# Attention denominators: two exponential tiles added by an accumulating DMA, one pass of the small constant over the sum

## What is computed

```python
scores = jnp.einsum('bhtd,bhsd->bhts', q, k) / SCALE
scores = jnp.where(causal[None, None], scores, NEG_INF)
attn = jax.nn.softmax(scores, axis=-1)
mask = jnp.clip((R + z[:, :, None, None] - dist) / R, 0.0, 1.0)
attn = attn * mask
attn = attn / (attn.sum(axis=-1, keepdims=True) + 1e-08)
out = jnp.einsum('bhts,bhsd->bhtd', attn, v)
```

## Time and profile before

| | |
|---|---|
| median of three runs | 3301.56 us (3301.55 to 3304.24) |
| the profiled execution | span 3301.3 us; the median of the runs is 0.3 us above it |
| self-attention | from 355 to 1825 us of the span, some 1470 us in eight iterations |
| busy in the span | PE 91%, DVE 56%, ACT 32%, POOL 29% |

### The profile page before, as it was taken

One profiled execution on the slowest core, in us unless ns is written; L12 is line 12 of the kernel. 1 busy time (PEld: TensorE's weight loads), 2 busy tenths in 40 slices (PEclk: granted clock), 3 DMA queues, 4 the chain that ended last, 5 costly groups with the idle time before them and its releaser, 6 DMA issues. The chain is left out here.

```text
span 3301.3 us, 54795 instructions
## 1 busy us (share of the span) xinstructions
PE 2990.0 (91%) x19242; PEld 1673.0 (51%) x19242; DVE 1859.6 (56%) x2220; ACT 1063.0 (32%) x2510; POOL 943.3 (29%) x606
## 2 busy tenths in 40 slices
PE   8998799999999999999999789999999787777778
PEld 6876333333333333333333678888888343333335
DVE  4355878787887878787883345555554510000038
ACT  3222344444444444444444223333333100101123
POOL 0000554445444444445454022222222000000013
PEclk9999899999999999999999889999999888878889
DMA  4453512121212212131200411111111669999954
GB/s 166 178 204 128 128 49 62 51 70 44 70 53 55 69 48 60 52 73 43 69 16 4 150 42 64 64 64 64 64 64 65 243 249 420 420 421 420 421 226 162
DMA packets 181219, 438.54 MB, mean 133 GB/s; under 512 B 17470, under 2 KB 51928, under 8 KB 156457
## 3 DMA queue, kind: packets, MB, share of 16 engines
q1 hardware_dynamic: 174057, 425.19, 36.8%
q10 hardware_dynamic: 6976, 10.75, 0.9%
HBM read 351.74 MB, written 83.89 MB: 132 GB/s over the span
## 5 line engine op out<-in xcount | busy, mean ns | idle before, releaser
L785 ACT ACTIVATE B_e<-B_pS 128x512 f32<-128x512 f32 (+3 forms) x1280 | 619.2, 534 | 850.0 <-PE B_pS L865 427.9
L640 POOL TENSOR_TENSOR B_em<-B_e,B_mask 128x1024 f32<-128x1024 f32 (+1 forms) x320 | 670.9, 2098 | 730.7 <-ACT B_e L785 693.9
L703 DVE TENSOR_REDUCE mx<-B_pM 128x4 f32<-128x2048 f32 (+2 forms) x299 | 588.9, 1969 | 38.7 <-PE B_pM L847 20.3
L865 PE MATMUL B_pS<-B_qs,B_ks 128*128 128x512 f32 (+3 forms) x1280 | 505.2, 447 | 43.4 <-issue 19.7
L696 DVE SCALAR_TENSOR_TENSOR B_em<-B_mask,B_e 128x1024 f32<-128x1024 f32 (+1 forms) x320 | 354.4, 1108 | 257.9 <-PE B_pN L895 256.3
L865 PEld LDWEIGHTS B_pS<-B_qs,B_ks 128*128 128x128 f32 x1280 | 227.8, 192 | 363.1 <-issue 238.5
L883 PE MATMUL B_pD<-B_e,B_tiny 128*32 128x512 f32 (+3 forms) x2560 | 310.0, 557 | 0.0
L889 PE MATMUL B_pD<-B_em,B_ones 128*32 128x512 f32 (+3 forms) x2560 | 301.2, 543 | 0.3 <-DVE B_em L696 0.3
L895 PE MATMUL B_pN<-B_em,B_v 128*32 128x512 f32 (+3 forms) x2560 | 293.4, 530 | 0.0
L2089 PE MATMUL E_pI<-ring,hT 128*32 128x512 f32 x1024 | 184.5, 815 | 101.1 <-DMA ring<-in_L_ffn_e_W_dram 57.8
L2012 DVE TENSOR_TENSOR E_ug<-E_pT,bT 128x32 f32 x32 | 5.7, 192 | 445.2 <-PE E_pT L2099 445.2
(11 more groups left out here) (288 smaller groups left out, 4764.2 us busy)
## 6 DMA issues: line engine op xcount, KB each, us to landing
ring<-in_L_ffn_e_W_dram SPq DMA_DIRECT2D x128, 1024.0 KB, 21.8
ring<-in_L_ffn_e_Wg_dram SPq DMA_DIRECT2D x64, 1024.0 KB, 23.6
B_qs<-q_hi SPq DMA_DIRECT2D x64, 256.0 KB, 4.5
B_ks<-k_hi SPq DMA_DIRECT2D x64, 256.0 KB, 3.9
E_xq<-xT_sc ACTq DMA_DIRECT2D x18, 512.0 KB, 10.3
ring<-x_sc SPq DMA_DIRECT2D x36, 256.0 KB, 2.6
qc<-in_x_dram SPq DMA_DIRECT2D x34, 256.0 KB, 2.7
qc<-a_sc SPq DMA_DIRECT2D x34, 256.0 KB, 3.0
```

Of the source, the lines that this page charges most:

```text
L640: nc.gpsimd.tensor_tensor(em[:, f % SLOTS_EM, DVE_HEADS:, w0:], e[:, f % SLOTS_E, DVE_HEADS:, w0:], mask[:, DVE_HEADS:, u0:u0 + BLK - w0], ...
L703: nc.vector.tensor_reduce(mx[:, :, qt, c], pM[:, :, 0:w], AX.X, ALU.max).then_inc(max_taken, 1)
L785: nc.scalar.activation(e[:, f % SLOTS_E, h, w0:], pS[:, h % SBANKS, w0:], ACT.Exp, scale=SCALE).then_inc(exp_ready, 1)
L865: last = nc.tensor.matmul(pS[:, h % SBANKS, w0:], ks[:, kb // NT, h, kb % NT * P:(kb % NT + 1) * P], qs[:, qb, h, w0:], start=True, stop=( ...
```

## The change

Full steps are taken in pairs (a, a+1) with a even: 4, 6, 12, 14, 16, 18, 24, 26, ..., 34, twelve in an iteration. GpSimd issues an accumulating transfer that adds the e of step a+1 onto the e of step a, in SBUF: 128 partitions of 2048 float32, 1 MB. It is issued ahead of GpSimd's `weigh` of step a+1, after em of step a has been made on both engines and the four exponentials of step a+1 are there. TensorE leaves out the round of `tiny` at steps a and a+1, and does one on the sum in the mix of step a+2 (`SUMMED_AFTER`), after a wait for the transfer. Steps on the diagonal keep their own round. e has five slots in place of four, and ScalarE's wait for a free slot now asks for the mix of step f-3, not of f-4.

```diff
--- before.py
+++ after.py
@@ -58,7 +58,8 @@
 
 KB = T // P
 SCALE = float(DH) ** -0.5
-SLOTS_E, SLOTS_EM = 4, 2
+SLOTS_E, SLOTS_EM = 5, 2
+E_KEPT = 3
 SBANKS = 2
 DVE_HEADS = 2
 DEN_EPS = 1e-8
@@ -67,6 +68,12 @@
 FLAT = [(qb, kb) for qb in range(BPB) for kb in range(NT * (qb + 1))]
 STEPS = len(FLAT)
 ENDS = [NT * (qb + 1) * (qb + 2) // 2 - 1 for qb in range(BPB)]
+PAIRS = [f for f, (qb, kb) in enumerate(FLAT) if kb < NT * qb and kb % 2 == 0]
+PAIRED = {f for a in PAIRS for f in (a, a + 1)}
+SUMMED_AFTER = 2
+TINY_AT = {f: [a for a in PAIRS if a + SUMMED_AFTER == f] + [f] * (f not in PAIRED) for f in range(STEPS)}
+PAIRS_BY = len(PAIRS) // 2
+assert len(PAIRS) % 2 == 0 and STEPS % SLOTS_E == 0
 UNITS = [(qb, qt, c) for qb in range(BPB) for c in [qb] + list(range(qb)) for qt in range(NT)]
 EARLY = 21
 EARLY_ROWS = sum(end < EARLY for end in ENDS)
@@ -508,6 +515,8 @@
         pD = ps("B_pD", [P, BLK], F32)
         sp_carried = sem("B_sp_carried")
         dve_carried = sem("B_dve_carried")
+        pool_carried = sem("B_pool_carried")
+        summed = [sem(f"B_summed{u}") for u in range(2)]
         made = sem("B_made")
         const_ready = sem("B_const_ready")
         spans_loaded = sem("B_spans_loaded")
@@ -640,6 +649,17 @@
                 nc.gpsimd.tensor_tensor(em[:, f % SLOTS_EM, DVE_HEADS:, w0:], e[:, f % SLOTS_E, DVE_HEADS:, w0:],
                                         mask[:, DVE_HEADS:, u0:u0 + BLK - w0], ALU.mult).then_inc(masked_last, 1)
 
+            def add_pair(it, a):
+
+                b, n = a + 1, PAIRS.index(a)
+                pool.wait_ge(masked, it * STEPS + a + 1)
+                carry(pool, pool_carried)
+                pool.wait_ge(masked_last, it * STEPS + a + 1)
+                carry(pool, pool_carried)
+                pool.wait_ge(exp_ready, it * HPG * STEPS + HPG * (b + 1) + SBANKS)
+                carry(pool, pool_carried)
+                pool.dma_start(e[:, a % SLOTS_E, :, :], e[:, b % SLOTS_E, :, :], accum_op=ALU.add).then_inc(summed[n % 2], 16)
+
             def divide(it, qb):
                 n = it * BPB + qb
                 pool.wait_ge(inverse, n * 2 + 2)
@@ -652,6 +672,8 @@
 
             def group(it, final):
                 for f in range(2, STEPS + 2):
+                    if f - 1 in PAIRS:
+                        add_pair(it, f - 1)
                     if not final or f < STEPS:
                         weigh(it, f)
                     if f - 5 in ENDS:
@@ -780,7 +802,7 @@
                 w0 = width(f)
                 for h in heads:
                     if h == 0:
-                        act.wait_ge(mixed, it * STEPS + STEPS + f + 1 - SLOTS_E)
+                        act.wait_ge(mixed, it * STEPS + STEPS + f + 1 - E_KEPT)
                     act.wait_ge(score_ready, it * HPG * STEPS + HPG * f + h + 1)
                     nc.scalar.activation(e[:, f % SLOTS_E, h, w0:], pS[:, h % SBANKS, w0:],
                                          ACT.Exp, scale=SCALE).then_inc(exp_ready, 1)
@@ -877,17 +899,24 @@
                     pe.wait_ge(v_loaded[qb], 16 * (it + 1))
                 if first:
                     pe.wait_ge(den_out, it * BPB + qb + 1)
-                pe.wait_ge(exp_ready, it * HPG * STEPS + HPG * (f + 1) + SBANKS)
-                for h in range(HPG):
-                    cols = slice(h * DH, (h + 1) * DH)
-                    nc.tensor.matmul(pD[cols, w0:], tiny[:, :], e[:, f % SLOTS_E, h, w0:],
-                                     start=first, stop=False, tile_position=(0, h * DH))
+                opened = not first
+                for a in TINY_AT[f]:
+                    n, at = PAIRS.index(a) if a in PAIRED else 0, width(a)
+                    if a in PAIRED:
+                        pe.wait_ge(summed[n % 2], 16 * (it * PAIRS_BY + n // 2 + 1))
+                    else:
+                        pe.wait_ge(exp_ready, it * HPG * STEPS + HPG * (f + 1) + SBANKS)
+                    for h in range(HPG):
+                        cols = slice(h * DH, (h + 1) * DH)
+                        nc.tensor.matmul(pD[cols, at:], tiny[:, :], e[:, a % SLOTS_E, h, at:],
+                                         start=not opened, stop=False, tile_position=(0, h * DH))
+                    opened = True
                 pe.wait_ge(masked, it * STEPS + f + 1)
                 pe.wait_ge(masked_last, it * STEPS + f + 1)
                 for h in range(HPG):
                     cols = slice(h * DH, (h + 1) * DH)
                     nc.tensor.matmul(pD[cols, w0:], ones[:, :], em[:, f % SLOTS_EM, h, w0:],
-                                     start=False, stop=final, tile_position=(0, h * DH))
+                                     start=not opened, stop=final, tile_position=(0, h * DH))
                 if first:
                     pe.wait_ge(num_out, it * BPB + qb + 1)
                 for h in range(HPG):
```

## The result

The changed kernel takes 3313.93 us (median of 6 runs, 3304.82 to 3321.68) against 3301.69 us before (6 runs, 3299.81 to 3304.24): 1.0045 times as long, interval 1.0031 to 1.0058. It is slower by about 12 us where 73 us less were forecast. The profiled execution has a span of 3316.9 us. Its runs scatter over 17 us, those of the kernel before over 4.

What follows compares the result with a forecast made beforehand. PE was taken to set the pace, in program order, except at an iteration's end. 3301.3 - 84.5 (rounds) + 3 (transfer) + 8 (VectorE) = 3227.8, so 3228 us; range 3212 to 3370, the forecast's own 3212 to 3240.

Steps and rivals of the forecast that it cites:

- The price of a round: PE's full steps: each removed round is worth 0.88 us, 84.5 us in all.
- The count of rounds: PE, per iteration: 24 rounds of tiny go, 12 on sums come; 96 fewer in the program.
- the waits and slots that were put at nothing: ScalarE's wait for a slot (mix of step f-3) and PE's waits on new semaphores: claimed to cost nothing.
- The transfer: GpSimd's add in SBUF: 6.8 us plus 1.0 for the issue, hidden, landing 1.3 us early; 3 us charged.
- its two added terms: Added to the sum: 3 us for the transfer, 8 us for VectorE's delay in iterations with ramps.
- The window of 9.1 us: Row 3, pair 32, 33: time from possible issue to the tiny round of step 34's mix, 9.1 us.
- Rival (A): Transfer lands after its need: 3356 us at 12 us to landing; chance 0.24 beyond break-even, 0.09 with part of the gain.
- What stands behind the transfer: Row 3: GpSimd's later product delays VectorE's ramps and maxima, 1.2 us in each of seven iterations, 8 us.
- g: GpSimd: the time it is held to issue one transfer, taken as 1.0 us, between 0.38 and 2.38.
- Rival (B): Row 3: VectorE becomes the bound, 35 us of the gain go, about 3255 us; chance 0.10.
- (C): GpSimd held far longer than 2.4 us by the issue: 3409 us at 5 us; chance 0.07.
- the issue's part in the lock on the ramps: VectorE and GpSimd: a page says they block each other, descriptor generation included; no run showed it for the issue.

Runs made afterwards that it cites:

- the four combinations: Changed kernel, transfer issued ahead of or behind GpSimd's product, sum's round at mix's head or end: ahead/head 3313.93, behind/head 3312.36, ahead/end 3300.26, behind/end 3239.48 us.
- the memset: Changed kernel without its transfers, GpSimd filling a small tile of its own where the issue stood: 3232.72 us, ratio 0.9803.
- the plain copies: Changed kernel with each accumulating transfer replaced by a plain copy of e issued by SyncE: 3220.78 us, ratio 0.9764.
- The two moves: Changed kernel with the transfer issued behind GpSimd's product and the round on a sum at the mix's end: 3239.48 us, ratio 0.9821.
- quarters: Kernel with issue behind and round last, plus VectorE's reciprocals after rows 0 to 2 in four pieces instead of two: 3238.08 us, ratio 0.9812.
- ramps first: Kernel with issue behind, round last and reciprocals in four pieces, plus VectorE's row 3 ramps ahead of its product: 3260.41 us, ratio 0.9885.

## Why the prediction was wrong, step by step

The price of a round was right: 0.88 us a round, 84.5 in all, and 80 us came in the kernel without transfers. The count of rounds was right, and so were the waits and slots that were put at nothing.

The transfer was right in the main. It lands 7.5 us after the issue's start; the sum had 6.8 and 1.0 for the issue. PE waits 10.6 us for it, where 3 were charged: under by 8 us, against the 97 by which the kernel misses the sum without its two added terms (3313.9 against 3301.7 - 84.5). The window of 9.1 us holds too: 2.4 us later, with the issue behind the product, the waits grow to 59.8 us. One premise under it was wrong: that GpSimd can issue when it could have begun its product, since both wait for the same exponentials. The issue also waits for VectorE's product of step a, and GpSimd was idle for it 34 times, up to 2.5 us. That is of little harm to the landing, but it makes GpSimd's own product late whenever VectorE is. Rival (A) did not happen, though it had most of the chance of a slower kernel. On the page that has an add at half of a copy's rate for its second read (the Trainium skill, Collectives: The Full Stack, section on the bandwidth ceiling) the runs show 7.5 us against 5.0 for a plain copy, from another queue: 1.5 times with all fixed parts in it, and no contradiction.

The step that failed is "What stands behind the transfer", the term of 8 us for VectorE; it came to about 80. The step moved GpSimd's product by g and followed this only through the ramps, which the rows showed waiting for GpSimd. VectorE's own product reads two operands from SBUF and waits the same way. The earlier trace rows has no such case (the product at 1070.84 starts behind the end of GpSimd's at 1069.97), but the trace before has it: at step 13 VectorE's product starts inside GpSimd's in all eight iterations, and takes 1.63 to 1.68 us, as here, until 1.08 us behind the end of GpSimd's:

```profile
961.86 2.38 POOL L640 TENSOR_TENSOR B_em<-B_e,B_mask 128x1024 f32<-128x1024 f32 x1 [3.04 <-ACT B_e L785]
...
963.64 1.68 DVE L696 SCALAR_TENSOR_TENSOR B_em<-B_mask,B_e 128x1024 f32<-128x1024 f32 x1
```

The step also left out what happens right after a row, where two reciprocals (1.74 us each) come on top. In the changed kernel VectorE arrives there late and starts its product into GpSimd's or into the issue ahead of it. The product then takes up to 4.2 us, once 5.58, and the delay goes on to PE by the maxima. Measured from the two stages: PE's waits on VectorE are 50 us more (80.8 + 23.6 against 38.8 + 15.7 without transfers), those for transfers 10.6 more, together 60.5 of the 60.9 us of idle time.

A second part was not in the sum at all: PE's clock falls to 1.2 GHz after some of these pauses, in 23 places against 8, and PE is busy for 29.4 us more with the same matmuls. 60.9 + 29.4 = 90.3 us, the whole difference of the stages.

Rival (B) had the right engine and too small a price: it put 1 us on each of five pairs, and only in row 3, 3255 us, while the worst place is in row 2. It counted VectorE's busy share (0.97 after the change) and not that a late instruction there gets longer. (C), GpSimd held too long, did not happen: its record of the issue is 0.88 us, and the product's record starts 0.6 us after the issue's. That the loss needs the issue ahead of the product is shown by the four combinations (61 us with the round at the end); that a later start of the product alone doesn't make it, by the memset (13 us), as far as it is a stand-in; and that the traffic of copies doesn't, by the plain copies (1.3 us). How much of the 61 us is the lock that begins with the issue, how much the product's 0.3 us of extra length, and how much GpSimd's wait for VectorE was not separated. Of the 20 us between 3239 and the 3219 without transfers the profiled stages have 19.3: 12.2 of idle time (10.6 of it waits for transfers) and 7.1 of busy time.

## What to carry to other kernels

When a shorter chain of matmuls takes the slack of another engine, ask what that engine's instructions will overlap once they start later, not only whether its work still fits: two engines that lock each other turn half a microsecond of delay into three. An instruction put ahead of another on a side engine is priced by who is locked behind both; here it cost 61 us less behind it, once the consumer was moved back as well. And an instruction that waits for another engine, put ahead of a product that did not, makes the product wait too. The two moves were worth 2 and 14 us singly and 74 together.

## What the runs showed of the hardware that was not expected

A product of VectorE that starts during GpSimd's issue of a transfer, with GpSimd's product right behind the issue, takes 4.17 to 4.21 us in all 8 cases of the changed kernel, and a ramp in this place 2.97 to 3.09 us in all 7; both end 1.09 and 0.29 us behind the end of GpSimd's product. One of the ramps:

```profile
1066.31 0.88 POOL L661 DMA_DIRECT2D B_e<-B_e  x1 [2.54 <-DVE B_em L718]
...
1066.90 2.97 DVE L695 TENSOR_SCALAR B_mask<-B_ndist,B_span 128x512 f32<-128x512 f32 x1
1066.92 2.66 POOL L649 TENSOR_TENSOR B_em<-B_e,B_mask 128x1024 f32<-128x1024 f32 x1
```

With no product right behind, the same issue holds nobody. In the kernel with the issue behind and the round last, 31 products of VectorE start during an issue, and all take 1.21 to 1.23 us, as this one:

```profile
962.00 0.86 POOL L661 DMA_DIRECT2D B_e<-B_e  x1
962.10 1.22 DVE L718 SCALAR_TENSOR_TENSOR B_em<-B_mask,B_e 128x1024 f32<-128x1024 f32 x1 [1.31 <-PE B_pD L911]
...
963.75 2.37 POOL L649 TENSOR_TENSOR B_em<-B_e,B_mask 128x1024 f32<-128x1024 f32 x1 [0.89 <-ACT B_e L807]
```

And with a product but no issue in progress, the one that starts first goes first. In 39 cases of the changed kernel VectorE's product starts 0.02 to 0.98 us ahead of GpSimd's while no issue has started, and takes 1.21 to 1.23 us, while GpSimd's is the longer one (2.52 to 3.40 us). In the 8 cases above it starts 0.42 to 0.44 us ahead of GpSimd's, and is held. One of the 39:

```profile
1060.34 1.22 DVE L718 SCALAR_TENSOR_TENSOR B_em<-B_mask,B_e 128x1024 f32<-128x1024 f32 x1
1060.67 3.10 POOL L649 TENSOR_TENSOR B_em<-B_e,B_mask 128x1024 f32<-128x1024 f32 x1 [1.11 <-ACT B_e L807]
```

So it is as if GpSimd's product held VectorE back from the moment it stands behind the issue, before its own record starts. This reading is argued from the rows; the rows themselves are shown. The longest product of all fits it: it starts inside the first of two products of GpSimd that follow each other at once, and ends 1.08 us behind the second, so that it got no turn in between:

```profile
1313.09 5.03 POOL L649 TENSOR_TENSOR B_em<-B_e,B_mask 128x1024 f32<-128x1024 f32 x2
1313.62 5.58 DVE L718 SCALAR_TENSOR_TENSOR B_em<-B_mask,B_e 128x1024 f32<-128x1024 f32 x1 [1.73 <-PE B_pN L924]
```

The product's record behind an issue is also longer, 2.67 us against 2.37. The Trainium skill, SBUF — State Buffer, "Who interferes with whom", has the lock between a VectorE instruction with two inputs in SBUF and a GpSimd one that reads SBUF, and the traces agree: VectorE's product ends 1.08 to 1.09 us behind GpSimd's when it starts inside it.

The prediction had no run for the issue's part in the lock on the ramps. Two of the runs have one: in the kernels with both moves and quarters, with and without ramps first, 14 ramps start during an issue that has no product right behind, and take 0.47 to 0.48 us, as ramps do alone. The issue's record is 0.87 to 0.93 us long in them, and the transfer lands 6.9 to 7.3 us after its start. Nothing of a lock shows on either side.

PE's clock: in the 3 us from 1066 in the changed kernel it is granted at 0.50, the 1.2 GHz level. Before that PE paused twice, for 1.11 us until 1064.04 and for 0.54 us until 1065.38:

```profile
1064.04 0.28 PE L856 MATMUL B_pM<-ident,B_mm 128*16 128x128 f32 x1 [1.11 <-DVE B_mm L728]
...
1065.38 0.33 PE L869 MATMUL B_pM<-kh,qh 32*128 32x128 f32 x4 [0.54 <-DVE B_mrow L734]
```

The window of the 3 us from 1066 (the granted clock is the last number but two):

```profile
1066.00:1069.00 3.00, 3.00 (x17) 1.04 (x18) 2.98 (x3) 1.08 (x2) 2.69 (x2) 0.50 0.46 96
```
